# First four scan tiles divided by ScalarE's Ln and Exp with a Newton step, and the next tile's scans placed between

## The reference, cut to what matters

```python
tf = sigmoid(sum(time_emb, -1))
decay = exp(-exp(w))[None, :] * (0.5 + 0.5 * tf)
ek = exp(minimum(k, 30.0)); ekv = ek * v
_, (nf, df) = lax.scan(step, init, (ekv_t, ek_t))                # a = a*decay + in, forward in time
_, (nb, db) = lax.scan(step, init, (ekv_t, ek_t), reverse=True)
euk = exp(minimum(u + k, 30.0))
num = nf + nb - ekv + euk * v
den = df + db - ek + euk
out = sigmoid(r) * (num / maximum(den, 1e-8)) * (0.8 + 0.2 * tf)
...
x = x + attention(cond(x, f, f, ...), Wq, Wk, Wv, Wo, betas)
```

## Time and profile before

| | us |
|---|---|
| median of 3 runs (lowest, highest) | 1583.58 (1582.86, 1585.2) |
| span of the profiled execution, first to last instruction | 1581.4 |
| what lies around the span, by the median | 2.2 |
| PE busy | 1547.0 (98%) |
| DVE busy | 1219.7 (77%) |
| ACT busy | 782.1 (49%) |
| POOL busy | 615.2 (39%) |
| mean granted TensorE clock | 0.999 |

### The profile page before, as it was taken

The page is one execution under the profiler, slowest core; times in us unless marked ns, Lnnn a source line. Parts: engine busy times, 40 slices in busy tenths (PEclk is TensorE's granted clock), DMA queues, the critical chain, the costliest instruction groups (busy, mean ns, idle before and its releaser), DMA issues.

```text
span 1581.4 us, 26868 instructions
## 1 busy us (share of the span) xinstructions
PE 1547.0 (98%) x9574; PEld 1377.9 (87%) x9574; DVE 1219.7 (77%) x2719; ACT 782.1 (49%) x1687; POOL 615.2 (39%) x433
## 2 busy tenths in 40 slices
PE   4899999999999999999999999999999999999999
PEld 2699989999999999998999999989888888888887
DVE  8889888787878888778775773665897888687785
ACT  3576566445535626535546552653554443344442
POOL 3666585322222222222001000134664465666662
PEclk9999999999999999999999999999999999999999
DMA  5375685595473485474467547348211222311111
GB/s 177 124 246 191 223 292 195 180 392 184 161 276 127 154 286 201 147 254 160 174 228 280 210 171 283 110 141 279 88 54 54 60 89 72 107 46 62 54 41 54
DMA packets 109381, 262.04 MB, mean 166 GB/s; under 512 B 11200, under 2 KB 36160, under 8 KB 107840
## 3 DMA queue, kind: packets, MB, share of 16 engines
q1 hardware_dynamic: 90384, 227.28, 40.5%
q10 hardware_dynamic: 18864, 33.04, 6.5%
HBM read 212.03 MB, written 48.25 MB: 165 GB/s over the span
## 4 chain that ended last, share of the span: by engine, by line
PE 90%; DVE 6%; issue 2%; DMA 1%; ACT 1%; POOL 0%; SPq 0%; ACTq 0%; DVEq 0%
PE psG L595 17%; PE psG L597 17%; PE psG L596 17%; PE psX L771 4%; PE psX L726 3%; PE psX L595 3%; PE psX L597 3%; PE psX L596 3%; PE psZ L752 3%; PE psZ L743 3%; PE psZ L751 2%; PE psZ L597 2%; PE psY L597 2%; PE psY L596 2%; PE psZ L596 2%
## 5 line engine op out<-in xcount | busy, mean ns | idle before, releaser
L2076 POOL TENSOR_TENSOR wl<-stage,wh 128x512 fp32r<-128x512 f32 x160 | 233.5, 1481 | 147.4 <-ACT wh L1597 144.7
L595 PE MATMUL psG<-yh,wh 128*128 128x512 f32 x646 | 263.1, 407 | 0.0
L597 PE MATMUL psG<-yh,wl 128*128 128x512 f32 x646 | 253.0, 392 | 0.0
L596 PE MATMUL psG<-yl,wh 128*128 128x512 f32 x646 | 252.1, 390 | 0.0
L2144 POOL TENSOR_TENSOR vs<-v,omb 128x512 f32<-128x512 f32 x64 | 92.1, 1460 | 388.9 <-PE psX L726 216.0
L597 PEld LDWEIGHTS psG<-yh,wl 128*128 128x128 f32 x646 | 121.3, 188 | 26.8
L595 PE MATMUL psG<-wh,yh 128*128 128x256 f32 x480 | 141.6, 295 | 0.0
L595 PEld LDWEIGHTS psG<-yh,wh 128*128 128x128 f32 x646 | 121.9, 189 | 20.9 <-DVE sg L1274 0.3
L596 PEld LDWEIGHTS psG<-yl,wh 128*128 128x128 f32 x646 | 121.9, 189 | 20.5
L597 PE MATMUL psG<-wh,yl 128*128 128x256 f32 x480 | 135.7, 283 | 0.0
L596 PE MATMUL psG<-wl,yh 128*128 128x256 f32 x480 | 135.7, 283 | 0.0
(11 more groups left out here) (279 smaller groups left out, 4291.6 us busy)
## 6 DMA issues: line engine op xcount, KB each, us to landing
wh<-high_o SPq DMA_DIRECT2D x52, 512.0 KB, 3.6
wl<-low_o SPq DMA_DIRECT2D x52, 512.0 KB, 4.7
stage<-in_w SPq DMA_DIRECT2D x64, 256.0 KB, 3.1
wh<-high_k SPq DMA_DIRECT2D x23, 512.0 KB, 3.7
wl<-low_k SPq DMA_DIRECT2D x23, 512.0 KB, 5.0
wh<-high_q SPq DMA_DIRECT2D x23, 512.0 KB, 4.1
wl<-low_q SPq DMA_DIRECT2D x23, 512.0 KB, 5.8
wh<-high_v SPq DMA_DIRECT2D x22, 512.0 KB, 4.0
```

The source lines that it names most:

```text
L595: e.matmul(out, lh, rh, start=first, stop=False, skip_group_check=check)
L596: e.matmul(out, lh, rl, start=False, stop=False, skip_group_check=check)
L597: return e.matmul(out, ll, rh, start=False, stop=last, skip_group_check=check)
L2076: e.tensor_tensor(lo, raw, hi, ALU.subtract).then_inc(p_wl, 1)
```

## The change

- For tiles 0 to 3 DVE's reciprocal goes (except the first half of tile 3, `rc0` and `rc1`). In its place ACT's new `recip(t)` takes Ln of the denominator and then Exp of minus that, r, into DBK (or sq). A Newton step follows: out = (2 - d r) (n r), with m = n r and step = d r as two products of POOL's new `newton(t)` (tile 0's m is DVE's `own_product`), and DVE's `oy` joins them.
- The factor `tf[2]` is folded into the sigmoid's sum: exp_r gets the bias ln(1/tf[2]), and adding 1/tf[2] moves from ACT to POOL (`one_more(t)`), with a cap at 1e14.
- DVE's order: tile t+1's `df` (and `nf` for t > 0) stand ahead of tile t's `oy`.
- POOL's waits on `v_d3` and `v_oh` are gone, and its list is in another order.
- The two stores of beta share one semaphore, and the second, bo, is computed after tile 1's denominator.

```diff
+LARGE = 1e14
+UNIT = 2.0 ** -37
+LN_UNIT = -37 * math.log(2.0)
...
                     if i == 0:
-                        if t < 4:
-                            w.wait_ge(a_e1, t + 1)
-                        else:
-                            w.wait_ge(p_er, er_count(t) - 4)
+                        w.wait_ge(p_er, er_count(t))
...
+                elif name == "oy" and t < 4:
+                    cut = slice(256 if t == 3 else 0, T)
+                    w.wait_ge(p_nr, products(t))
+                    if t == 0:
+                        w.wait_ge(v_rc, 1)
+                    m, _, step, _ = newton_of(t)
+                    e.scalar_tensor_tensor(oys[t][:, cut], step, 2.0, m, ALU.subtract, ALU.mult,
+                                           reverse0=True).then_inc(v_oy, 1)
...
+            scan(0, "d2")
+            scan(0, "d3")
+            scan(0, "n2")
+            w.wait_ge(a_c, 5)
             e.tensor_scalar_add(bt, bt, 1.0).then_inc(v_c, 1)
+            mn(2)
+            w.wait_ge(v_c, 13)
             e.reciprocal(br, bt).then_inc(v_c, 1)
+            own_product()
+            scan(1, "df")
+            scan(0, "oy")
+            scan(1, "nf")
+            scan(1, "db")
+            for name in ("nb", "d2", "n2", "d3"):
+                scan(1, name)
+            mu(2)
+            mn(3)
+            mu(3)
+            w.wait_ge(v_c, 14)
             e.tensor_scalar(bo, br, -1.0, 1.0, ALU.mult, ALU.add).then_inc(v_c, 1)
-            first_tile(1)
-            first_tile(2)
-            first_tile(3)
+            for t in (2, 3):
+                scan(t, "df")
+                scan(t, "nf")
+                scan(t - 1, "oy")
+                for name in ("db", "nb", "d2", "n2", "d3"):
+                    scan(t, name)
+            scan(3, "rc0")
+            scan(3, "rc1")
+            first_half()
+            scan(3, "oy")
+            w.wait_ge(p_c, 6)
+            e.reciprocal(later[3], later[1]).then_inc(v_c, 1)
...
                     if t < 4:
-                        w.wait_ge(a_er, t + 1)
-                        e.activation(er_of(t), er_of(t), ACT.Identity, bias=1.0).then_inc(a_e1, 1)
+                        w.wait_ge(a_c, 4)
+                        e.activation(er_of(t), er_of(t), ACT.Exp, scale=-1.0, bias=ln_over).then_inc(a_er, 1)
...
+            def recip(t):
+
+                _, d, _, r = newton_of(t)
+                w.wait_ge(v_d3, t + 1)
+                e.activation(r, d, ACT.Ln, scale=UNIT).then_inc(a_rc, 1)
+                w.wait_ge(a_rc, 2 * t + 1)
+                e.activation(r, r, ACT.Exp, scale=-1.0, bias=ln_unit).then_inc(a_rc, 1)
...
+            def newton(t):
+
+                m, d, step, r = newton_of(t)
+                w.wait_ge(a_rc, 2 * t + 2)
+                w.wait_ge(v_n2, t + 1)
+                if t > 0:
+                    e.tensor_tensor(m, m, r, ALU.mult).then_inc(p_nr, 1)
+                e.tensor_tensor(step, d, r, ALU.mult).then_inc(p_nr, 1)
...
             ekv(0)
-            w.wait_ge(v_d3, 1)
             euv(0)
+            one_more(0)
             ekv(1)
             euv(1)
+            newton(0)
+            one_more(1)
+            ekv(2)
+            low_y(0)
             later_rates()
-            for t in range(2, 4):
-                w.wait_ge(v_d3, t)
-                ekv(t)
-                euv(t)
-                low_y(t - 2)
+            newton(1)
+            euv(2)
+            one_more(2)
+            ekv(3)
+            low_y(1)
+            newton(2)
+            euv(3)
+            one_more(3)
+            low_y(2)
+            newton(3)
```

More of the change, by code:

```diff
@@ L1 @@
+import math
 from contextlib import ExitStack
@@ L522, in adaln_attn_ffn, with newton_of, products @@
         ones = S[:, 0, 0:P]
+        over_tf, ln_over, ln_unit = tf[:, 0, :], tf[:, 3, 0:1], tf[:, 3, 1:2]
+        def newton_of(t):
+            cut = slice(256 if t == 3 else 0, T)
+            nf, df, nbk, dbk, _, _ = set_of(t)
+            return nf[:, cut], df[:, cut], nbk[:, cut], dbk[:, cut]
+        def products(t):
+            return 2 * t + 1
         bt, br, bo = (S[:, 1, 16 * i:16 * i + 16] for i in range(3))
@@ L1306, in gains, with own_product @@
                 e.tensor_tensor(first[2], first[0], first[3], ALU.mult).then_inc(v_c, 1)
[L1308 to L1333, removed]
+            def own_product():
+                m, _, _, r = newton_of(0)
+                w.wait_ge(a_rc, 2)
+                w.wait_ge(v_n2, 1)
+                e.tensor_tensor(m, m, r, ALU.mult).then_inc(v_rc, 1)
             def first_half():
@@ L1614, in exp_r @@
                     w.wait_ge(sem, value)
-                    e.activation(er_of(t), er_of(t), ACT.Exp, scale=-1.0).then_inc(a_er, 1)
                     if t < 4:
-                        w.wait_ge(a_er, t + 1)
-                        e.activation(er_of(t), er_of(t), ACT.Identity, bias=1.0).then_inc(a_e1, 1)
+                        w.wait_ge(a_c, 4)
+                        e.activation(er_of(t), er_of(t), ACT.Exp, scale=-1.0, bias=ln_over).then_inc(a_er, 1)
+                    else:
+                        e.activation(er_of(t), er_of(t), ACT.Exp, scale=-1.0).then_inc(a_er, 1)
+            def recip(t):
[4 more added lines that the diff above has]
+                e.activation(r, r, ACT.Exp, scale=-1.0, bias=ln_unit).then_inc(a_rc, 1)
             def ends_of(t):
@@ L1818, in load_beta @@
                 g = n % NG
-                w.wait_ge(d_b[0], 16)
+                w.wait_ge(d_b, 32)
                 w.wait_ge(v_t2, 6 * n)
@@ L1856, in scalar @@
             exp_u(0)
[L1857 to L1871, removed]
+            w.wait_ge(v_c, 12)
+            e.activation(ln_over, over_tf[:, 0:1], ACT.Ln).then_inc(a_c, 1)
+            ends_of(0)
+            w.wait_ge(d_bt, 16)
+            e.activation(bt, bt, ACT.Exp, scale=-1.0).then_inc(a_c, 1)
+            exp_k(1)
+            exp_r(0)
+            exp_u(1)
+            recip(0)
+            exp_k(2)
+            exp_r(1)
+            ends_of(1)
+            high_y(0)
+            recip(1)
+            exp_u(2)
+            exp_k(3)
+            exp_u(3)
+            load_ombeta(0)
+            load_beta(0)
+            exp_r(2)
+            ends_of(2)
+            high_y(1)
+            recip(2)
+            load_k(4)
+            exp_r(3)
+            ends_of(3)
+            high_y(2)
+            recip(3)
+            load_k(5)
             load_r(3)
@@ L2376, in sync @@
             e.dma_start(mask[:, :], mask_d).then_inc(d_id, 16)
-            w.wait_ge(v_c, 14)
-            e.dma_start(spread(beta_s[0]), br).then_inc(d_b[0], 16)
-            e.dma_start(spread(beta_s[1]), bo).then_inc(d_b[1], 16)
+            w.wait_ge(v_c, 15)
+            e.dma_start(spread(beta_s[0]), br).then_inc(d_b, 16)
+            e.dma_start(spread(beta_s[1]), bo).then_inc(d_b, 16)
             load_w(2)
```

57 lines of the change are left out of this document (32 added, 25 removed).

## The result

The median went from 1582.99 to 1593.96 us (five runs each, 1582.86 to 1585.2 and 1592.83 to 1596.15): +11.0 us, ratio 1.0067, 95% interval 1.0055 to 1.008. The forecast was 1591.1, that is slower by 7.5; the sign and the mechanism held and 3.5 us were missing. The profiled execution has a span of 1592.1 us beside 1581.4.

The account below looks back on a forecast made before the run. PE, 98% busy, was taken as bound by DVE's start through tile 3's second half. Tiles 3.4, 3.0, 1.8 late, 1.1 gained, plus PE's chunk gave +7.9 or +7.3, taken +7.5: 1588.9 span, 1591.1 median; range 1582 to 1595.

Parts of the forecast that it names:

- likeliest case: Whole kernel: +4 to +9 us, own range 1587.5 to 1593, chance 0.58.
- the signs that were named for it: PE's first chunk near 23.4, third near 51.7, second half 61.5 to 63.6; scans 2.2, steps 1.7, loads 1.28 us.
- longer ACT chain: Rival on ACT: the load ahead of Ln isn't hidden, or beta loads stall ACT; +9 to +12 us, chance 0.10.
- Tile 0: First tile of the start: 1.0 + 1.2 + 1.2 = 3.4 us late, its oy at 23.4.
- two and a bit: 1.2 us up to d3: Tile 0, DVE: charge for ekv(1), the sigmoid's sum and euv(1) falling on d2, d3 and n2.
- unknown costs: Bounds: about ten clashes (end +4 if DVE wins three), slower Ln +0.3, Ln loads only after d3, near +11.
- ten clashes at 1.0: Start, tiles 0 to 3: about ten POOL products meeting DVE instructions, each costing DVE 1.0 us.
- Tile 3 and PE: Tile 3's first half 1.1 us gained; PE's chunk 2 takes 9.0, first half 2.85, second half starts at 63.5.
- Hidden load, two issues of beta: ACT: load ahead of Ln runs while waiting for d3; beta's loads land under DVE's wait for oy(1), charged 0.
- The rival in which that cover is gone: Beta's loads no longer covered by DVE's wait cost 1 us; beta stalling ACT is in a rival of +9 to +12, chance 0.10.
- "Faster" rival: Start: removed reciprocals count in full, POOL's products fall in DVE's waits; 1581.5 to 1579.7 us, chance 0.14.
- The forecast's objection to it: Per tile, DVE's 8.1 us and POOL's some 5.5 exclude each other: 13.6 where the kernel before needs 11.5.

Follow-up runs that it names:

- e1: Changed kernel with POOL's sum of the sigmoid made without the minimum (multiply by 1.0, then add the column 1/tf[2]); 1593.19 us, ratio 1.0059 to the kernel before.
- e4: Changed kernel with the sigmoid's sum back on ACT, without a minimum, and none on POOL; 1590.78 us, ratio 1.0045 to the kernel before.
- e8: Kernel before with ACT's division only for tile 3's second half, Newton's products on DVE, a PE v product moved later; 1582.13 us, ratio 0.9993.
- f1: Kernel before with ACT's division, no Newton step, POOL's products held until d3, caps in DVE's wait, tile 3's ending reordered; 1579.49 us, ratio 0.9978.
- e3: Kernel before without POOL's waits that hold its products until DVE's reciprocals start, no division changed; 1592.05 us, ratio 1.0051.
- e2: Changed kernel with POOL's sum keeping the minimum but adding a constant 1.0 instead of the column; 1592.86 us, one run.

## Why the prediction was right, and where it fell short

- **The number: in the range, beyond the likeliest case.** +11.0 lies outside the forecast's own case of +4 to +9, and the starts of chunk 0, chunk 2 and the second half (25.91, 54.51, 65.79) all lie later than the signs that were named for it. The wide range holds the time because it also took in part of the "longer ACT chain", and that rival's mechanism didn't happen. The other signs came: scans of 2.2, steps of 1.7, DVE's waits for POOL's product, loads of 1.28.
- **What bounds: right.** The start is DVE's but for PE's last 1.4 us, and nothing later absorbed the shift: +10.16 at the second half, +10.7 at the end. (Of the idle times that the prediction adds up, the first, 2.48, was ended by a DMA and not by DVE's oy.)
- **Tile 0: the step that failed.** The forecast let PE start at 23.4; it was 25.91. The term that was mis-sized is "two and a bit: 1.2 us up to d3". It holds the sigmoid's sum as one clash among three and no wait for it; a minimum and a sum on POOL took 2.44 us. d2 lost nothing, d3 waited 1.97 for the sum and then lost 1.0 to ekv(1): 2.9 in place of 1.2. e1 and e4, with a shorter sum or none on POOL, start PE's chunk 0 earlier by 1.3 and 0.4 beyond the profile's start. db was 1.2 late for 1.0, and the whole profile starts 0.34 later. From d3's end to PE's start the forecast had 6.5 and the trace has 25.91 - 19.19 = 6.7. Tile 0 makes 2.2 of the 3.5 us that were missing. (The others: 0.3 for the start, 0.3 in tile 2, 0.4 for the choice of 7.5, 0.5 later in the kernel, 0.3 more in the medians than in the spans, less 0.6 on PE.) The unknown costs had no bound for it either: they ask about clashes, Ln and the loads, and the sum, whose operation had changed, isn't among them.
- **Tile 1: right.** 14.89 us against 14.9 (38.3 - 23.4), with a wait of 2.32 where 2.3 was forecast.
- **Tile 2: right, 0.3 short.** 13.71 against 13.4 (51.7 - 38.3), with a wait of 3.04 for 2.7. The ten clashes at 1.0 were ten, nine of them ahead of PE's third chunk, and three of 0.4, not all at the places that were named.
- **A slip in the sums.** Tile 1's parts, 9.9 + 3.0 + 2.3, are 15.2 and not 15.1, and 23.4 + 15.1 is 38.5 and not 38.3. The three latenesses, 3.4 + 3.0 + 1.8, would put chunk 2 at 52.1 and not at 51.7, and the whole 0.4 higher. By its parts the forecast has 28.7 us for tiles 1 and 2 together, where 28.6 were measured; that the 14.9 fits to the hundredth is luck.
- **Tile 3 and PE.** As forecast, PE is what holds the second half: DVE's last oy is done at 64.36 and PE busy until 65.79. Chunk 2 took 8.69 for 9.0, the first half 2.59 for 2.85, so the second half came 2.3 after its 63.5. But the two prices were misread from the kernel before. Its 8.87 was put down to the clock, and e8 takes the same 8.87 at a clock of 1.00; its 2.85 is the distance of DVE's two half oys, and PE without a pause takes 2.59. That 9.0 came near the 8.69 of the slow clock is luck. Taking 7.5 in place of the sum's own 7.9, because the clock might be full, was wrong by 0.4: the clock was at 0.50 from 55 to 58.
- **The rest,** 0.5 us of PE's time spread over the later kernel, wasn't forecast and isn't explained.
- **Hidden load, two issues of beta:** no wait on either shows. The rival in which that cover is gone gave a time near the measured one, for a reason that isn't there.
- **"Faster" rival:** its mechanism, that the freed time counts once the products stand where DVE waits, is what f1 builds. The forecast's objection to it holds for the order in the change only, not for an order that holds the products back.

## What to carry to other kernels

Before an engine's slow step is moved away, ask what ran in its shadow. Here DVE's reciprocals were the only stretch of a tile in which POOL could work without taking time from DVE, and e3 shows that this cover alone is worth 9 us in the kernel before. Replace a wait or a step together with the semaphore that puts the neighbour's work under it. And take no operation at the price of its neighbour: an added minimum made a sum twice as long.

## What the runs showed of the hardware

- A minimum and a sum over 128x512 fp32 took POOL 2.24 to 2.88 us in the changed kernel and e2, a product and a sum 1.11 to 1.58 in e1. Yet the minimum and sum of 2.30 us cost a scan beside it only 0.43 us (40.67), and the product and sum of 1.11 in e1 (38.70) cost it 0.44. Of the longer one 1.94 us were left when the scan began, so it doesn't hold what they share to its end.
- DVE's reciprocal with one input loses nothing to POOL, but a cap with one input does (1.43 for 0.47 in e3). One input is no sign of safety.
- Each Ln and each Exp after it has a table load of 1.28 us in the built program. The Trainium skill ("ScalarE: Activation LUTs", table sets) speaks of one set with both; no run here shows that one.
- Ahead of chunk 2 PE had no work for 2.8 to 6.0 us, and in all kernels but e8 the granted clock stood at 0.50 for a part of the chunk: from 45 to 48 in the kernel before and from 55 to 58 in the changed one, where it was 1.00 at the first product, and from 52.5 to 59 in e1 and from 40 to 46.5 in f1, where it had fallen before the chunk began. In e8, after 3.1 us without work, it stayed at 1.00. A saving ahead of such a chunk can be lost there, as in e1.
